# The next batch's maxima moved within the key tile loops of an attention tower, on TensorE and VectorE

## The reference

```
qp = q @ w.T;  kp = k @ w.T;  vp = v @ w.T          # 128 channels, 7200 keys
scores = einsum("bqd,bkd->bqk", qp, kp) / sqrt(128)
attn = softmax(scores, axis=2)
out = einsum("bqk,bkd->bqd", attn, vp)
out = layernorm(out @ fc_w.T + fc_b + q) * gamma + beta
...
router_probs = softmax(x @ router_w.T + bias);  topk_p, topk_i = top_k(router_probs, 6)
```

## Time and profile before

| | |
|---|---|
| median of 3 runs | 1650.11 us (1646.83 to 1660.38) |
| profiled execution, its own time | 1647.7 us |
| its span | 1645.9 us |
| TensorE busy | 1529.1 us, 93% |
| TensorE weight loads busy | 1018.1 us, 62% |
| VectorE busy | 1052.4 us, 64% |
| ScalarE busy | 721.6 us, 44% |
| GpSimd busy | 559.5 us, 34% |
| mean granted TensorE clock | 0.979 |

### The profile page before, as it was taken

The page is one execution under the profiler, slowest core; times in us unless marked ns, Lnnn a source line. Parts: engine busy times, 40 slices in busy tenths (PEclk is TensorE's granted clock), DMA queues, the critical chain, the costliest instruction groups (busy, mean ns, idle before and its releaser), DMA issues. The chain is left out here.

```text
span 1645.9 us, 30649 instructions
## 1 busy us (share of the span) xinstructions
PE 1529.1 (93%) x11598; PEld 1018.1 (62%) x11598; DVE 1052.4 (64%) x2087; ACT 721.6 (44%) x1269; POOL 559.5 (34%) x603
## 2 busy tenths in 40 slices
PE   2889998998997789999998999899999999999998
PEld 2556765765665447777777777678885444444444
DVE  4755545545234887776867777765565876877766
ACT  2231222222122126555554555456665665465554
POOL 2110001001004834602370235100795654555555
PEclk9999999999999879999999999999999999999999
DMA  8320100100001733602240223100122443344443
GB/s 218 89 89 23 29 26 17 29 26 21 1 1 53 184 88 78 143 1 73 59 123 21 65 72 94 37 23 2 54 85 88 131 130 92 123 136 132 138 130 107
DMA packets 142651, 124.74 MB, mean 76 GB/s; under 512 B 86613, under 2 KB 123949, under 8 KB 141485
## 3 DMA queue, kind: packets, MB, share of 16 engines
q1 hardware_dynamic: 127053, 110.62, 24.8%
q0 software_dynamic: 1152, 8.39, 1.6%
q10 hardware_dynamic: 14304, 3.81, 1.2%
HBM read 102.54 MB, written 5.28 MB: 66 GB/s over the span
## 5 line engine op out<-in xcount | busy, mean ns | idle before, releaser
L1186 DVE TENSOR_REDUCE region_c<-ps 120x1 f32<-120x512 f32 x336 | 225.6, 688 | 110.3 <-PE ps L1607 107.0
L873 ACT ACTIVATE region_c<-ps 128x720 f16<-128x720 f32 (+1 forms) x228 | 175.3, 769 | 274.5 <-PE ps L1637 274.5
L745 POOL TENSOR_TENSOR region_k<-region_c,region_k 128x480 f16<-128x480 f32 x198 | 217.1, 1100 | 174.0 <-ACT region_k L960 173.9
L1179 DVE TENSOR_TENSOR region_c<-ps,region_c 128x720 f16<-128x720 f32 (+1 forms) x228 | 206.1, 904 | 90.4 <-ACT ps L874 86.5
L1507 PE MATMUL ps<-region_k 128*128 128x360 f16 (+1 forms) x752 | 240.6, 320 | 5.2 <-ACT m L852 5.2
L1509 PE MATMUL ps<-region_k 128*128 128x360 f16 (+1 forms) x752 | 240.0, 319 | 0.0
L1508 PE MATMUL ps<-region_k 128*128 128x360 f16 (+1 forms) x752 | 239.7, 319 | 0.0
L665 POOL TENSOR_TENSOR vare<-mv,eps 120x6 f32<-120x6 f32 x20 | 4.0, 198 | 631.3 <-DVE mv L1111 631.3
L1654 PE MATMUL ps<-region_k,region_c 128*120 128x129 f16 (+1 forms) x1368 | 179.9, 221 | 0.0
L1655 PE MATMUL ps<-region_k,region_c 128*120 128x128 f16 (+1 forms) x1368 | 179.2, 220 | 0.0
L874 ACT ACTIVATE ps<-ps 128x720 f32<-128x720 f32 (+1 forms) x228 | 174.5, 766 | 0.0
(11 more groups left out here) (232 smaller groups left out, 2730.6 us busy)
## 6 DMA issues: line engine op xcount, KB each, us to landing
gates<-gates_dram SPq DMA_DIRECT2D x384, 120.0 KB, 2.8
region_c<-in_k SPq DMA_DIRECT2D x56, 256.0 KB, 2.7
region_c<-in_v SPq DMA_DIRECT2D x56, 256.0 KB, 2.9
region_c<-in_WcT POOLq DMA_DIRECT2D x8, 1024.0 KB, 6.4
region_c<-in_experts SPq DMA_DIRECT2D x18, 352.0 KB, 2.9
gates<-band_dram SPq DMA_DIRECT2D x26, 189.0 KB
region_k<-region_c SPq DMA_TRANSPOSE x120, 2.8
region_c<-in_xw SPq DMA_DIRECT2D x26, 63.0 KB
```

Of the source, the lines that this page charges most:

```text
L745: g.tensor_tensor(a_lo[u], ac[u], a_hi[u], ALU.subtract).then_inc(s["a_lo_ready"], 1)
L873: a.activation(halves(p_hi[u][0:parts]), st, ACT.Exp).then_inc(s["p_hi_ready"], 1)
L1179: v.tensor_tensor(halves(p_lo[u][0:parts]), two(2 * u, parts), halves(p_hi[u][0:parts]), ALU.subtract).then_inc(s["lo_ready"], 1)
L1186: v.tensor_reduce(mxk[:, r, bass.ds(c + 1, 1)], bank(bk, P), AX, ALU.max).then_inc(s["mx_free"], 1)
```

## The change

On TensorE, in the even slot, A goes between the first four and the last four matmuls of the score tile, and B between the high and the low products of `weigh`. C stays behind the odd slot's score tile. On VectorE, B's reduction goes behind the steps of the even tile (`prepare_second`). The maxima and their order among each other stay the same, as do the bank and the semaphores.

```diff
-                for r in ((0, 1), (2,), (3, 4), (5,))[part]:
-                    maximum_of(b, c, r)
+                maximum_of(b, c, (0, 2, 3, 5)[part])
+
+            def prepare_second(b, c, part):
+
+                if part % 2 == 0:
+                    maximum_of(b, c, (1, None, 4)[part])
...
                         if isinstance(i, int):
                             for x in beside(b, "dve", 8 * i + t):
                                 step(*x)
+                        if b + 1 < B:
+                            prepare_second(b + 1, 2 * i + t // 4, t % 4)
...
-            def key_scores(b, t, u, parts=KW):
+            def key_scores(b, t, u, parts=KW, row=None):
...
                     mm(bank(2 * u + w, parts)[:, 0:HALF], kh, q_lo[:, b, q], start=False, stop=False)
+                if row is not None:
+                    maximum_of(b + 1, *row)
                 for w in range(2):
...
-            def weigh(b, t, u, parts=KW):
+            def weigh(b, t, u, parts=KW, row=None):
...
                     mm(sums(r, C), ph, vl, start=False, stop=False, skip_group_check=True)
+                if row is not None:
+                    maximum_of(b + 1, *row)
                 pe.wait_ge(s["lo_ready"], TILES * b + t + 1)
...
                     for t in range(8):
+                        u = t // 4
+                        first, second, third = (((i, u, 3 * (t // 2 % 2) + k) if b + 1 < B else None) for k in range(3))
+                        early = first if t % 2 == 0 else None
                         if last and t == 7:
                             key_scores(b, KT, 0, TAIL)
                         else:
-                            key_scores(b, 8 * i + t + 1, (t + 1) % 2)
-                        u = t // 4
-                        if b + 1 < B:
-                            maximum_of(b + 1, i, u, (0, 2, 3, 5)[t % 4])
-                        weigh(b, 8 * i + t, t % 2)
-                        if b + 1 < B:
-                            if t % 2 == 0:
-                                maximum_of(b + 1, i, u, (1, None, 4)[t % 4])
+                            key_scores(b, 8 * i + t + 1, (t + 1) % 2, row=early)
+                        if third and t % 2:
+                            maximum_of(b + 1, *third)
+                        weigh(b, 8 * i + t, t % 2, row=second if t % 2 == 0 else None)
```

## The result

The changed kernel takes 1623.07 us (1619.72 to 1623.92, 4 runs) against 1649.53 (1646.83 to 1660.38, 4 runs) for the kernel before: a ratio of 0.983, with an interval of 0.9805 to 0.9854. The two profiled executions, on which all that follows rests, differ by less: 1647.7 and 1623.9, so 23.8 us (their spans 1645.9 and 1621.8).

The account below looks back on a forecast made before the run. TensorE, busy for 93% of the span, was taken to bound the kernel, so gains come from its waits. Terms 15.2 + 2.9 + 2.0 = 20.1 us saved, 1650.1 - 20 = 1630 us, range 1624 to 1642.

Parts of the forecast that it names:

- (1): TensorE, even tiles: A and B inserted earlier, taken as 0 us, bound 3.4 us gained or lost over 84 pairs.
- (2): VectorE, even tiles' steps ahead of B's reduction: odd tiles' low products stop waiting, steps free to 1.25 us; 15.2 us gained.
- (3): TensorE: B newly waits for A's reduction, 0.04 us to spare; taken as 0, bound 4 x 0.43 us a batch.
- (4): Waits outside the pair: second `fc` matmuls lose theirs, 2.9 us gained; GpSimd's 4 waits shrink about 0.5 each, 2 us.
- a pair without steps still takes 5.17 us: Sign of a right forecast: an even and an odd tile with no router step keep their 5.17 us.
- The first: Rival: B waits for A's reduction in every pair; at 0.1 us late, 12 us saved, 1638; chance 13%.
- The second: Rival: moved maxima expose their weight loads on TensorE, 0.10 us each; 16.8 us lost, 3 saved, 1647; chance 5%.
- The third: Rival: GpSimd's waits grow by 0.61 us and bring nothing; 15.7 us saved, 1634; chance 7%.
- The fourth: Rival, slower: even tile's `low_part` or A's reduction stretches by 0.43 us; 33 us lost against 20 gained, 1663; chance 5%.

Follow-up runs that it names:

- e3: VectorE's new order with A alone moved on TensorE, B left behind the low products, against the kernel before: 1623.59 us, ratio 0.9852.
- e1: The kernel before with TensorE's two moves alone, VectorE in its old order: 1642.94 us, ratio 0.9962.
- e2: The kernel before with VectorE's new order alone, the maxima at their old places on TensorE: 1626.54 us, ratio 0.9861.
- e12: The changed kernel with three extra VectorE steps (1.73 us) on each even tile: 1716.49 us, ratio 1.0412 to the kernel before.
- e8: The changed kernel with two extra VectorE steps on each odd tile: 1702.55 us, ratio 1.0318 to the kernel before.
- e11: The changed kernel itself, run again as the yardstick: 1625.02 us, ratio 0.9851 to the kernel before.

## Why the prediction was off by a little

Terms of the sum, as the profiled executions have them. The low products' term is what is left of each loop's gain (2.55, 11.51, 11.29) when 28 x 0.04 and the two other terms are taken off:

| | forecast | measured |
|---|---|---|
| (1) insertions on TensorE | 0 | 0.04 x 84 = 3.4 |
| (2) low products' waits, with (3) | 15.2 | 1.4 + 7.4 + 7.2 = 16.0 |
| (4) `fc` | 2.9 | 1.5 x 2 = 3.0 |
| (4) GpSimd's waits | 2.0 | (0.98 - 0.04 - 0.2) x 4 = 3.0 |
| batch 3's loop (0.9 of it the clock) | 0 | -1.3 |
| sum | 20.1 | 24.1 |

**The step that failed** is in (1): "I take 0, as one leaves a cheap place and the other the dear one." The bound of 3.4 us beside it was right and the whole of it came, as a gain. I had read 0.24 and 0.36 in the earlier trace rows as what a place costs. They were what B's wait for A's reduction costs: e3 leaves B at that place and has 0.22 and 0.34. The rows held the evidence. 0.44 to the reduction, 0.69 for it and 0.13 behind it, all used in (2), add up to 1.26, and A to B is 1.25. I worked that sum out for the new place of B, in (3), and not for the old one. The view of waits couldn't show it, as it lists nothing that small. What the runs showed in place of the 0 is 5.17 - 5.13 = 0.04 us in each of 84 pairs, 3.4 us gained. With it went the sign "a pair without steps still takes 5.17 us".

**(2) was right**, in mechanism and nearly in size. TensorE's order alone left 3.6 us of waits and VectorE's order alone took nearly all away (e1, e2). The steps of tiles 32 (the logits), 34 (the exponentials' sum) and 40 (`share`) cost 0.03, 0.17 and 0.40 in batch 1 where 0.22, 0.14 and 0.58 were forecast: tiles 32 and 40 find VectorE ahead and have the longer margin that e12 shows, and tile 34 the quiet one. In batch 2 it is tile 34 that finds VectorE ahead and waits not at all, while the load behind tile 32 waits 0.43. Tile 38 adds 0.05. The 16.0 is a remainder and no count of waits: in the kernel before, a low product's wait cost its pair some 0.07 more than the load's wait shows (5.46 against 5.17 us, with a wait of 0.21). The low products wait nowhere, where up to three places were allowed.

**(3) was right in its mechanism, and 0 was a little too good.** Beside odd steps of 0.70 the pairs take 5.18 or 5.19, so 0.05 to 0.06 and not 0.03 each; in 23 of the 84 pairs B starts 0.15 us behind A's reduction, so it is held by it. The odd step that a meeting with GpSimd stretched to 1.04 cost 0.40, as the bound of 0.43 said; there was one such in batch 1, not four. e8 gives 0.52 for a step of 1.1, as the margin says.

**(4)**: `fc` as forecast. At GpSimd's waits 0.9 us is left of each, as "about 1 us" said; of the head start 0.74 came through and not 0.5, since the aggregates are released 1.6 us earlier in the slot (4.04 to 2.44 us behind its start), not 1.27: the odd tile ahead ends earlier on VectorE as well.

**The rivals.** The first (B late in every pair) was in a way the truth of the kernel before: B was late there, by 0.02, and not after. The second (loads exposed) is excluded by 5.13 us for the pair: an inserted maximum costs 0.22 us at each place. The rule of the Trainium skill beside it ("TensorE: Matmul & The Clock Gate", section "The mechanism") isn't borne out by the trace here, as far as it makes a load wait wherever the row groups are the same. The same section also lets a load run ahead if it targets a background weight buffer, and no run here can tell whether these do. The third (GpSimd's waits grow) didn't happen. The fourth (neighbours stretch) didn't either: `low_part` reads 0.91 and the reduction 0.68 beside the score tile.

**The range** failed on its lower end, 1624 against 1623.07. It took in the 3.4 us of (1) from 1630 down to 1626.6, and 2.6 us for the spread of runs; the GpSimd term's bound of 1.3 each, written in (4), would have taken it 3 us further and was left out of the forecast's own bounds. Of the 26.5 us between medians 2.7 are the spread of runs, as the profiled executions differ by 23.8. The miss took both: without the 3.4 us, or without the 2.7, the median would have lain inside, and the same kernel as e11 took 1625.02, inside too. So that it fell 0.9 us outside is in part chance; the 0 in (1) was wrong all the same. The chance of 0.70 on faster by over 1% was on the right side: 1.7%.

## What to carry to other kernels

Work moved into the idle time that an engine has between two of its fixed duties costs nothing up to a margin that a quiet stretch of the trace gives: here VectorE's steps between two reductions, 20 of the 25 us that the three loops lost, with no instruction saved. Before a place on an engine is priced by the spacing of its instructions, the round trip of the resource that it uses (here one bank: matmul, reduction, next matmul) must be added up for the order as it is; if it equals the spacing, the spacing is a wait, though no view lists one. Where a waiting instruction stands decides whose steps are free: ahead of the low products it left the odd tiles 0.67 us, behind them the even tiles alone are limited, and A moved without B gave the same time with more to spare.

## What the runs showed of the hardware

- A maximum of 512 columns put between other matmuls costs 0.22 us from start to start wherever it stands, with its own load of weights hidden, and 0.24 where that load comes late. The round trip of one bank through VectorE is 1.26 us (0.42, 0.69, 0.15).
- A VectorE addition with both inputs in SBUF took 0.56 us alone and up to 1.51 beside GpSimd, mean 0.65, and GpSimd's cast went from 0.61 to 0.94 beside it. "SBUF — State Buffer", section "Who interferes with whom", of the Trainium skill names this pair as a conflict; the trace agrees, and the price is more than double the 0.43 that the prediction took from the earlier trace rows.
- Stretches of about 3.4 us at the 1.2 GHz level fall at other places from one profiled execution to another, of the same kernel as well. One of them in a loop that no edit touched made it 0.9 us longer (136.87 against 135.94).
